# Regrouping the pair products of a recommendation model in three sets, with the dense work of the first chunk laid around its last lots

## The reference, cut to what matters

```python
bot_out = _mlp(dense_x, [bw0, bw1, bw2], [bb0, bb1, bb2])            # 13 -> 512 -> 256 -> 128
gathered = jnp.stack([emb[t][sparse_x[:, t]] for t in range(26)], axis=1)
features = jnp.concatenate([bot_out[:, None, :], gathered], axis=1)  # 512 x 27 x 128
Z = jnp.einsum('bnd,bmd->bnm', features, features)
x = jnp.concatenate([bot_out, Z[:, LI, LJ]], axis=1)                 # 128 + 351 columns
return _mlp(x, [tw0, tw1, tw2, tw3, tw4], [tb0, tb1, tb2, tb3, tb4]) # 479 -> 1024 -> 1024 -> 512 -> 256 -> 1
```

## Time and profile before

| | |
|---|---|
| time, median of 3 runs | 181.64 us (181.28 to 182.43) |
| span of the profiled execution, first to last instruction | 179.6 us |
| what lies between the span and the median | 2.0 us |
| PE busy | 167.0 us, 93% of the span |
| POOL busy | 100.7 us, 56% |
| DVE busy, ACT busy | 82.2 us (46%), 66.3 us (37%) |
| mean granted TensorE clock | 0.991 |

### The profile page before, as it was taken

The page is one execution under the profiler, slowest core; times in us unless marked ns, Lnnn a source line. Parts: engine busy times, 40 slices in busy tenths (PEclk is TensorE's granted clock), DMA queues, the critical chain, the costliest instruction groups (busy, mean ns, idle before and its releaser), DMA issues.

```text
span 179.6 us, 3315 instructions
## 1 busy us (share of the span) xinstructions
PE 167.0 (93%) x1354; PEld 128.6 (72%) x1354; DVE 82.2 (46%) x177; ACT 66.3 (37%) x103; POOL 100.7 (56%) x112
## 2 busy tenths in 40 slices
PE   1999999899599994999999999989999999999993
PEld 1335557568377783798878889977888898788992
DVE  3202588955165756374452346343506625411422
ACT  0576748664143655133033253112504611110211
POOL 3777776777777777777777777767772000000000
PEclk9999999999999999799999999999999999999999
DMA  4999972434499733242232244422223120000000
GB/s 97 369 337 391 390 239 58 100 66 89 89 302 374 285 79 86 54 100 68 44 61 51 52 105 85 93 46 62 46 59 72 24 53 7 4 0 0 0 0 4
DMA packets 10124, 19.93 MB, mean 111 GB/s; under 512 B 5639, under 2 KB 5771, under 8 KB 9981
## 3 DMA queue, kind: packets, MB, share of 16 engines
q1 hardware_dynamic: 6636, 12.89, 22.0%
q0 software_dynamic: 3328, 6.82, 16.7%
q10 hardware_dynamic: 144, 0.00, 0.0%
HBM read 18.26 MB, written 1.44 MB: 110 GB/s over the span
## 4 chain that ended last, share of the span: by engine, by line
PE 71%; DMA 10%; POOL 8%; issue 4%; SPq 2%; DVE 2%; ACT 2%; POOLq 0%; DVEq 0%; ACTq 0%
PE acc L799 14%; PE acc L803 13%; PE acc L800 12%; POOL rows L420 8%; PE feat L781 6%; PE turned L944 5%; PE feat L763 5%; DMA rows<-in_emb,index 3%; PE turned L881 3%; DMA pairs<-pair_scratch 3%; DMA pair_scratch<-dots 3%; PE acc L829 2%; PE acc L938 2%; PE feat L938 2%; DMA v<-in_bw 1%
## 5 line engine op out<-in xcount | busy, mean ns | idle before, releaser
L420 POOL DMA_INDIRECT rows<-in_emb,index x104 | 99.5, 957 | 34.4 <-issue 30.0
L799 PE MATMUL acc<-w1h,y_split 128*128 128x512 f32 x64 | 27.9, 436 | 0.0
L803 PE MATMUL acc<-w1h,y_split 128*128 128x512 f32 x64 | 26.1, 407 | 0.0
L800 PE MATMUL acc<-w1l,y_split 128*128 128x512 f32 x64 | 25.5, 399 | 0.0
L444 ACT COPY featT<-feat 128x512 f32<-128x512 f32 x16 | 17.6, 1097 | 14.4 <-PE feat L763 14.3
L457 ACT ACTIVATE y_split<-turned 128x512 fp32r<-128x512 f32 x16 | 9.7, 606 | 35.1 <-PE turned L881 35.1
L651 DVE SCALAR_TENSOR_TENSOR y_split<-turned,y_split 128x512 fp32r<-128x512 f32 x16 | 11.1, 692 | 18.7 <-ACT y_split L457 18.7
L799 PE MATMUL acc<-w2h,y_split 128*128 128x256 f32 x64 | 18.8, 294 | 0.0
L803 PE MATMUL acc<-w2h,y_split 128*128 128x256 f32 x64 | 18.0, 281 | 0.0
L763 PE MATMUL feat<-ident,rows 128*128 128x128 f32 x104 | 15.3, 277 | 2.7 <-DMA rows<-in_emb,index 2.7
L800 PE MATMUL acc<-w2l,y_split 128*128 128x256 f32 x64 | 17.8, 279 | 0.0
(11 more groups left out here) (107 smaller groups left out, 255.6 us busy)
## 6 DMA issues: line engine op xcount, KB each, us to landing
w1r<-in_w SPq DMA_DIRECT2D x8, 512.0 KB, 13.8
w2r<-in_w SPq DMA_DIRECT2D x4, 512.0 KB, 6.0
rows<-in_emb,index POOLq DMA_INDIRECT x104, 3.0
w0r<-in_w_pairs SPq DMA_DIRECT2D x3, 512.0 KB, 7.8
top<-in_top_rows SPq DMA_DIRECT2D x1, 1024.0 KB, 12.1
pair_scratch<-dots SPq DMA_DIRECT2D x8, 104.0 KB, 2.3
pair_scratch<-dots SPq DMA_DIRECT2D x8, 71.5 KB
v<-in_bw SPq DMA_DIRECT2D x1, 512.0 KB, 3.6
```

The source lines that it names most:

```text
L420: pool.indirect_dma_start(rows[:, i, :], None, table, bass.IndirectOffsetOnAxis(ap=index[:, c, i:i + 1], axis=0)).then_inc(s_gather[LOTS * ...
L799: nc.tensor.matmul(dst, ah, wh, start=first, stop=False)
L800: nc.tensor.matmul(dst, ah, wl, start=False, stop=False)
L803: return nc.tensor.matmul(dst, al, wh, start=False, stop=end)
```

## The change

**Three sets.** The 27 features are cut in sets of 11, 11 and 5. Tile 0 now holds the 121 products between the first two sets, tile 1 the 110 products of the first two sets with the last and 16 within the last, tile 2 the 110 products within the first two sets and the bias row. Tiles 0 and 1 are copied from `dots` to `pairs` inside SBUF, with no way through DRAM. Only tile 2 goes through the scratch tensor. Tile 0's transfer (`across_out`) is issued on ACT's queue, right behind ACT's copies of `dots`; the others stay on SP's.

**Order.** PE runs `layer0(c, 1, 0)` and, from chunk 1 on, `layer3(c - 1)` ahead of `layer0(c, 0, 1)`. In chunk 0 the last two lots of chunk 1 are turned between the first steps of layer 2. ACT and DVE follow. `keep_going` ahead of chunk 0 has 8 matmuls and not 11, and there are 5 new ones behind chunk 0.

**Gathers.** A semaphore `s_go` is raised by the first matmul of `dots_of`; four waits for its last matmul (`s_z`) are now waits for this one, at earlier gathers.

**End.** In the last chunk layer 3's bias is added by a matmul with a row of ones (`bias3_in`), and DVE instead of ACT adds the last bias. The indices take three DVE steps and not four.

```diff
-TILE_FEATS = FEATS // PAIR_TILES
-PAIR_ROWS = TILE_FEATS * HOPS
+SET = 11
+LAST = FEATS - 2 * SET
+PAIR_ROWS = [SET * SET, 2 * SET * LAST + (LAST - 1) * (LAST - 1), 2 * SET * HOPS]
...
+        def across_out(eng, c, h):
+            eng.wait_ge(s_za, HALVES * c + h + 1)
+            eng.wait_ge(s_zd, HALVES * c + h + 1)
+            after(eng, s_xlp, PAIR_TILES * c)
+            eng.dma_start(pair_rows(h, 0, 0, PAIR_ROWS[0]), products(h, SET, SET, 0, SET)).then_inc(s_pin[h][0], 16)
...
+        DOTS_FIRST = (19, 28)
+        DOTS_SECOND, DOTS_LATER, DOTS_REST = 10, 12, 20
...
             def pairs_back(c, h):
-                sp.dma_start(scratch[h, 0:FIRST_ROWS], dots[low:mid]).then_inc(s_scr0[h], 16)
-                sp.dma_start(scratch[h, FIRST_ROWS:], dots[mid:low + FEATS]).then_inc(s_scr1[h], 16)
+                for t in range(2):
+                    sp.dma_start(scratch[h, t], products(h, t * SET, SET, t * SET, SET_COLS)).then_inc(s_scr[h], 16)
+                sp.dma_start(pair_rows(h, 1, 0, both), products(h, 0, 2 * SET, 2 * SET, LAST)).then_inc(s_pin[h][1], 16)
+                sp.dma_start(pair_rows(h, 1, both, PAIR_ROWS[1] - both),
+                             products(h, 2 * SET, LAST - 1, 2 * SET + 1, LAST - 1)).then_inc(s_pin[h][1], 16)
+                sp.wait_ge(s_scr[h], 32 * (c + 1))
...
             def fill_pace(g):
+                if g == DOTS_FIRST[0]:
+                    pool.wait_ge(s_go, 1)
+                if g == DOTS_FIRST[1]:
+                    pool.wait_ge(s_go, 2)
-                if g == 20:
-                    pool.wait_ge(s_z, 1)
-                if g == 31:
-                    pool.wait_ge(s_z, 2)
             def chunk_pace(c, i):
+                if i == (DOTS_SECOND if c == 0 else DOTS_LATER):
+                    pool.wait_ge(s_go, 2 * c + 3)
+                if i == DOTS_REST:
+                    pool.wait_ge(s_go, 2 * c + 4)
...
             def dots_out(c, h):            # ACT
                 nc.scalar.copy(*dot_quadrant(h, 1)).then_inc(s_za, 1)
+                across_out(act, c, h)
...
             def layer3_out(c):             # DVE
+                if c == CHUNKS - 1:
+                    before = layer3_block(c)
+                else:
+                    before = y3
+                    nc.vector.tensor_tensor(y3, layer3_block(c), bias3, ALU.add).then_inc(s_y3, 1)
...
+            def bias3_in(c):
+                nc.tensor.matmul(layer3_block(c), ones, bias3[0:1, :], start=False, stop=False)
...
-            keep_going(turned[0], 11)
+            keep_going(turned[0], 8)
             def chunk(c):                  # PE
                 layer0(c, 0, 0)
                 if c > 0:
                     turn2(c - 1, 1)
+                layer0(c, 1, 0)
+                if c > 0:
+                    layer3(c - 1)
                 layer0(c, 0, 1)
                 layer0(c, 0, 2, end=True)
-                if c > 0:
-                    layer3(c - 1)
-                layer0(c, 1, 0)
...
+                if c == 0:
+                    layer1(c, 1, 6)
+                    layer1(c, 1, 7)
+                    layer2(c, 0, range(0, 2), hi_ready(1, c, 0))
                     turn_lot(c + 1, 1, 2)
+                    layer2(c, 0, range(2, 4))
                     turn_lot(c + 1, 1, 3)
+                    pe.wait_ge(s_e[1], 2 * c + 2)
+                    layer2(c, 1, range(0, 2))
                     dots_of(c + 1, 1)
+                    turn(1, c, 1)
+                    layer2(c, 1, range(2, 4))
...
+                if c == 0:
+                    keep_going(acc_of(1, 0), 5, w0h[:, 0, :])
```

More of the change, by code:

```diff
@@ L55, in pair_order, with within @@
 def pair_order():
-    tiles = []
-    for i in range(PAIR_TILES):
-        for p in range(PAIR_ROWS):
-            n, h = i * TILE_FEATS + p // HOPS, p % HOPS
-            if n == FEATS - 1:
-                a, b = n, HOPS + h
-            elif n + h + 1 < COLS:
-                a, b = n + h + 1, n
-            else:
-                a, b = n + 1, n + h + 1 - COLS
-            tiles.append((a, b))
-    return tiles
+    def within(base, flat):
+        return base + flat // SET_COLS, base + flat % SET_COLS
+    across = [(SET + n, m) for n in range(SET) for m in range(SET)]
+    last = [(n, 2 * SET + m) for n in range(2 * SET) for m in range(LAST)]
+    last += [(2 * SET + n, 2 * SET + 1 + m) for n in range(LAST - 1) for m in range(LAST - 1)]
+    inside = [within(base, n * SET + 1 + h) for base in (0, SET) for n in range(SET_COLS) for h in range(HOPS)]
+    inside += [within(base, SET_COLS * SET_COLS + HOPS + h) for base in (0, SET) for h in range(HOPS)]
+    return [across, last, inside]
 def pair_weights(w, bias):
     out = np.zeros((PAIR_TILES, P, w.shape[1]), w.dtype)
-    for at, (a, b) in enumerate(pair_order()):
-        out[at // PAIR_ROWS, at % PAIR_ROWS] = w[DIM + a * (a - 1) // 2 + b]
-    out[PAIR_TILES - 1, PAIR_ROWS] = bias
+    placed = set()
+    for i, rows in enumerate(pair_order()):
+        for row, (n, m) in enumerate(rows):
+            a, b = max(n, m), min(n, m)
+            if a != b and (a, b) not in placed:
+                placed.add((a, b))
+                out[i, row] = w[DIM + a * (a - 1) // 2 + b]
+    assert len(placed) == FEATS * (FEATS - 1) // 2
+    out[PAIR_TILES - 1, PAIR_ROWS[PAIR_TILES - 1]] = bias
     return out
@@ L169, in rec_kernel @@
         ident_r = xl[:, 0, :]
+        ones = rows[0:1, 0, :]
         y3 = y_evac[:, 1, 0:T3]
@@ L428, in _ @@
                         gather_lot(c, h, j)
+            pool.wait_ge(s_ft, HALVES * LOTS * (CHUNKS - 1) + 1)
+            pool.memset(ones, 1.0).then_inc(s_ones, 1)
         @block.scalar
@@ L926, in layer3 @@
                 layer3_lo(c, 0)
+                if c == CHUNKS - 1:
+                    bias3_in(c)
                 layer3_hi(c, 1)
```

157 lines of the change are left out of this document (85 added, 72 removed).

## The result

The changed kernel takes 187.18 us in the median of 4 runs (186.69 to 190.15); the kernel before beside it takes 181.46. The ratio is 1.031, 95% interval 1.026 to 1.035. (Ratios are of fast runs; the 190.15 us is a run in a slower state that some executions fall into.) The forecast was 182.5 with a range up to 184.2: the change is slower, and slower than the range allows.

The account below looks back on a forecast made before the run. PE and POOL were taken as nearly even, with gathers about 1.25 us apart and POOL waiting for PE in a loop. +1.4 - 0.5 = +0.9 on a span of 179.6 gave 180.5, a time of 182.5 us, range 180.3 to 184.2.

Parts of the forecast that it names:

- First waits: POOL in chunk 0: gathers 20 to 27 come 0.52 us earlier, gather 28 and all up to 64 come 0.5 later.
- Last lots of chunk 0: Gather 51 starts at 69.3; PE, 1.6 us ahead, still waits for rows; products at 73.05, a gain of 1.6.
- Start of chunk 0: Direct copy of tile 0 and less work ahead of the turning let layer 1 start about 1.6 us earlier.
- ACT holds the turned half: Ahead of `split_hi` ACT waits 0.15 us and issues a 0.78 us transfer; PE stands about 2.3; gain so far 1.45.
- Five matmuls: The five new matmuls ahead of chunk 1 lie uncovered and cost 1.15 us; chunk 1 starts at 82.9.
- Layer 0 reordered: Half 0 ends 4.55 us behind the chunk's start, gather 65 starts 1.4 later, layer 1 starts 7.05 behind.
- Chunks 1 and 2: Late gathers delay chunk 2 by 0.75 us and chunk 3's start by 1.4; gathers 74 and 100 at most 0.4 each.
- What would show it: List of expected trace signs, among them PE waiting 0.9 us for rows at the last lots of chunks 1 and 2.
- The end: Last chunk: layer 3's addition goes, the bias matmul costs 0.1 us at most, DVE's step is shorter; together -0.5.
- The clock falls in chunk 0's new idle time: Rival: PE's waits near 79 us bring the low clock in layer 2, 1.3 us more, 183.8; chance 0.23.
- The gathers do not follow half 0: Rival: the 0.80 us behind half 0 is mostly POOL's overhead, or other holds loosen; -1.8, 180.7; chance 0.22.
- PE's order wins: Rival: chunk 0's waiting and slow clock go, PE is never caught by last lots; 178.7; chance 0.09.

Follow-up runs that it names:

- experiment 8: Kernel before with only the new waits for the products' first matmul, in place of those for the last: 186.92 us, 1.031.
- 16: Kernel before with one wait changed: gather 46 waits for the products' first matmul, in place of gather 51 for their last: 184.54 us, 1.019.
- 1: Changed kernel without any waits that pace gathers, new or old: 183.52 us, 1.015.
- experiment 3: Changed kernel with part of the weights (two pieces of `w2`, and `top`) loaded later, after layer 0 of chunk 0 is turned: 185.13 us, 1.021.
- 2: Changed kernel with the old waits for the products' last matmul in place of those for the first: 185.35 us, 1.025.
- experiment 15: Changed kernel with one wait moved from gather 46 to gather 51: 187.69 us, 1.039.
- 6: Changed kernel without pacing waits, ACT rounding layer 1's turned second half before starting tile 0's transfer: 181.41 us, 1.001.
- experiment 7: Changed kernel without pacing waits, ACT's transfer behind the rounding, PE's old order of layer 0, no five matmuls: 180.98 us, 1.000.
- experiment 14: Changed kernel without pacing waits, ACT's transfer behind the rounding, no five matmuls, DVE adding layer 3's bias before copying layer 0's half 0: 179.75 us, 0.992.
- 18: The kernel of experiment 14 with the five matmuls ahead of chunk 1 put back: 179.54 us, 0.993.
- 4: Changed kernel with 7 and 3 dummy matmuls filling PE's waits for rows at lots 2 and 3 in chunk 0: 187.01 us, 1.034.
- 13: Kernel before without any of the waits that only pace gathers: 180.65 us, 0.998.

## Why the prediction was wrong

**The steps that failed are "First waits" and "Last lots of chunk 0".** They follow gathers 28 and 51 and never ask what gather 46's new wait does. I had moved PE 1.6 us ahead for layer 1 of chunk 0 and carried that lead through to the last lots, past two lots of the first half that stand in between. For a gather's landing I had only the 2.9 us of the earlier trace rows, a place without bulk loads, and did not look at the stretch from 50 to 62 us, where it was 5.7 to 6.5 already in the kernel before. There a PE that comes earlier meets gathers that go later (gather 28, and all behind it, 1.4 later; 0.5 told, and up to 0.7 of it by the late `v`), and it had to wait 2.46 us. The lead became a lateness, matmuls ran at the lower clock, the first products began 3.27 later than before, gather 46 waited for them, and gather 51 came at 72.63 and not at 69.3. The second products were foretold at 73.05 and began at 76.76. Of the 5.2 us that the span lies above the forecast, 3.7 are in place when chunk 1 begins (86.56 against 82.9), up to 1.1 of them from the late `v`.

What the runs show of this mechanism: the new waits alone cost 3.1% in the kernel before (experiment 8), the one at gather 46 1.9% (16), part of both by a lower clock that sets in ahead of gather 46. Without any pacing wait the changed kernel keeps 1.5% (1), and its chunk 1 then begins at 82.71, where the forecast had it. The late rows are shown by experiment 3: with the loads moved, the landing time, the wait and the lateness of the first products are gone. That gather 46 is the wait that matters within the changed kernel is **not** shown: with the old waits in its place the changed kernel still loses 2.5% (2), in experiment 3 it is not held and 2.1% are lost, and experiment 15 decides nothing. What these have in common is gather 65, held 3.1 and 3.3 us by half 0 of layer 0, and 2.4 in the trace of 15; how much that wait costs alone was not tried. The parts don't add up: against no pacing waits at all, the new set costs 3.4% in the old order (1.031 over 0.998) and 1.6% in the new (1.031 over 1.015).

**"Start of chunk 0"** was right: from the second products to layer 0 it is 6.57 us and not 8.40, to layer 1 11.98 and not 13.81, a gain of 1.8 (1.6 told).

**"ACT holds the turned half"** was right in place and size: ACT's issue 0.85 (0.78 told), the wait for DVE's copies ahead of it 0.30 (0.15), PE idle 1.71 and 0.23 (2.3 told). Moving both behind the rounding took 1.3% off (6), of which the trace shows 1.1 us ahead of chunk 1 and 0.64 in chunks 1 and 2. The row was the better guide here. The Trainium skill (DMA: Bandwidth & Descriptors, Issuing engines are not separate DMA queues) calls the sequencer's time for starting a DMA usually small relative to the DMA itself. This case's trace does not bear that out for a transfer of 30 KB: in chunk 0 ACT's issue took 0.83 us, and ACT could round the tile 2.9 us after the issue's start (43.62 to 46.53).

**"Five matmuls"** stood bare in the trace (1.18 us, 1.15 told), but in time their removal can't be seen (0.993 against 0.992). Chunk 1 does begin 1.20 us earlier without them (80.40 in experiment 7, 81.60 in 6). Where it is given back is not shown: the trace of experiment 14 lost time to rows near 58 us and that of 18 did not, so the two can't be compared.

**"Layer 0 reordered"** was right: half 0 ended 4.62 behind the chunk's start (4.55 told), layer 1 began 7.13 behind (7.05), gather 65 went 0.79 behind half 0 (0.80). The sum had the wait for DVE in it and took it for a part of PE's new order. It comes from DVE's list, 0.51 us in each of three chunks: mended there, it gives 0.8% (1.001 to 0.993).

**"Chunks 1 and 2"**: the distances grew by 1.32 and 0.98 us, told were 1.05 and 0.65. The sizes are near, the make-up is not: PE waited for rows at the last lots for only 0.48 and 0.22 us, where "What would show it" has 0.9 each. The 1.32 is 0.36 up to the first products (layer 0's order), 0.69 between the products (with the 0.48 in it) and 0.27 behind them (ACT's issue; experiment 6 takes it away). Gathers 74 and 100 were held 0.33 each, within the bound of 0.4. But experiment 8 shows what kept that so small: in the old order the same waits hold gathers 74 and 100 for 2.1 and 1.7.

**"The end"** gave 0.01 and not 0.5: from layer 3's first matmul to the issue of the result it is 4.24 us (179.96 to 184.20), before 4.25 (173.90 to 178.15). PE's timeline after:

```profile
180.97 0.50 PE L946 MATMUL feat<-w3h,y2l 128*128 128x256 f32 x2
181.40 0.69 PE L955 MATMUL feat<-top,rows 1*128 1x256 f32 x2
182.03 0.38 PE L939 MATMUL feat<-w3h,y2h 128*128 128x256 f32 x1
```

From layer 3's low products (180.97) to its next high ones (182.03) it is 1.06 us, before 0.58 (174.92 to 175.50 in the timeline of PE). The bias matmul costs 0.48 bare, as much as the addition that it replaces (0.46); 0.1 was told. A single row of float32 was not cheap here.

**The rivals.** "The clock falls in chunk 0's new idle time" named the right kind of event and the wrong place: near 62 us and not near 79, and 1.6 us over 15 matmuls where it had 1.3. Whether the low clock makes part of the loss or only goes with it is open: filling the wait bought no time (4), but in experiments 1, 4 and 15 the executions with the highest mean clock are the shortest. "The gathers do not follow half 0" did not happen (0.79 behind it), and "PE's order wins" did not either.

## What to carry to other kernels

When a pacing wait is moved to another event, list every instruction that gets it and compare, in the trace, the event's time with the instruction's own; one that is a tie (62.33 and 62.40 here) is a wait from then on. The release alone took 0.6 to 1.1 us from the event's start, and whatever makes the producer late now makes the transfers late that it needs next. Take the landing time of a small transfer from the stretch in which it will run, not from a quiet one; the trace of before has it. A transfer's issue belongs behind the work that another engine waits for, and an order that lies on three engines must be undone on all three before an experiment says anything of it.

## What the hardware showed unexpectedly

- A gather beside bulk loads near 390 GB/s took 6.6 us to its use, 2.8 elsewhere; with part of the loads moved away (experiment 3) those of the same stretch landed in 3.2.
- The low clock near 50 us came in the traces of experiments 8, 13 and 16 (0.72 from 48 to 54 us) and not in that of the kernel before (1.00), behind nearly the same idle time of PE: 1.78, 1.92, 1.83 and, in the kernel before, 1.94 us. What differs earlier is that in those three PE had also stood 1.1 to 1.6 us for rows near 32 and 38 us, in the kernel before 0.22. Why the clock fell stays open.
- Between the start of the first product and the gather that waits for it lay 0.59 us in the changed kernel (40.31 to 40.90, 65.60 to 66.19) and 1.08 and 1.09 in the kernel before with the new waits (63.64 to 64.72, 102.93 to 104.02), 0.58 there for gather 28. Told was 0.45. Why two values occur stays open.
- A matmul of one row in float32 onto 256 columns held PE 0.48 us longer, where the products of rounded parts (fp32r) over 128 rows are 0.12 apart.
